# Graph attention over 25,000 edges: node pairs placed in the edge pipeline's first slots, small tables loaded in parts, and the segment sum in two passes

## What is computed

```
q = (x @ Wq + bq); k = (x @ Wk + bk); v = (x @ Wv + bv)        # 8 heads of 32
e = edge_attr @ We
kj = k[src] + e
alpha = einsum('ehc,ehc->eh', q[dst], kj) / sqrt(32)
ea = exp(alpha - segment_max(alpha, dst)[dst])
alpha = ea / (segment_sum(ea, dst)[dst] + 1e-16)
out = segment_sum((v[src] + e) * alpha[:, :, None], dst) + (x @ Ws + bs)
result = layernorm(x + out)
```

## Time and profile before

| | |
|---|---|
| median of 3 runs | 1380.74 us |
| the profiled execution | 1379.87 us, of which the span from first to last instruction is 1377.7 us |
| mean granted TensorE clock | 0.978 |
| busy: PE / PEld | 1297.1 us (94%) / 1157.9 us (84%) |
| busy: DVE / POOL / ACT | 974.1 us (71%) / 807.3 us (59%) / 729.4 us (53%) |
| node part, PE | until about 381 us |
| edge part, PE | 392.9 to about 1338 us |

### The profile page before, as it was taken

One profiled execution on the slowest core, in us unless ns is written; L12 is line 12 of the kernel. 1 busy time (PEld: TensorE's weight loads), 2 busy tenths in 40 slices (PEclk: granted clock), 3 DMA queues, 4 the chain that ended last, 5 costly groups with the idle time before them and its releaser, 6 DMA issues.

```text
span 1377.7 us, 26634 instructions
## 1 busy us (share of the span) xinstructions
PE 1297.1 (94%) x8027; PEld 1157.9 (84%) x8027; DVE 974.1 (71%) x2950; ACT 729.4 (53%) x1972; POOL 807.3 (59%) x749
## 2 busy tenths in 40 slices
PE   5689999999969999999999999999999999999973
PEld 4568888888859999899999999999999999999962
DVE  4497777777747777777777777767777777777763
ACT  2345555555535555555655555555555555555540
POOL 1123222222275677677777777777777777777542
PEclk9799999999989999999999999999999999999995
DMA  6769888888763344444444444444445444444310
GB/s 160 215 213 325 307 304 305 305 304 305 289 201 108 95 105 111 101 115 110 115 117 116 118 114 120 121 118 119 119 119 126 116 121 127 113 124 121 92 53 25
DMA packets 97231, 216.69 MB, mean 157 GB/s; under 512 B 31469, under 2 KB 35201, under 8 KB 97056
## 3 DMA queue, kind: packets, MB, share of 16 engines
q1 hardware_dynamic: 68672, 145.63, 33.1%
q0 software_dynamic: 28416, 69.35, 19.8%
HBM read 145.17 MB, written 77.90 MB: 162 GB/s over the span
## 4 chain that ended last, share of the span: by engine, by line
PE 91%; DVE 4%; DMA 3%; issue 1%; ACT 0%; POOL 0%; SPq 0%; POOLq 0%; DVEq 0%; ACTq 0%
PE bank L953 50%; PE bank L933 22%; PE bank L945 7%; PE bank L965 6%; PE bank L978 2%; PE bank L962 2%; DMA xT<-xt_dram 2%; DVE y L667 1%; PE bank L1022 1%; DVE y L681 1%; PE bank L990 1%; DVE at L653 1%; DMA rows_in<-xrows_dram,slot 1%; DMA bias<-bs_dram 1%; PE bank L984 0%
## 5 line engine op out<-in xcount | busy, mean ns | idle before, releaser
L403 POOL DMA_INDIRECT rows_in<-xrows_dram,slot x392 | 413.7, 1055 | 119.9 <-issue 94.6
L933 PE MATMUL bank<-w_y,xT 128*128 128x256 f32 x1568 | 345.9, 384 | 35.2 <-DMA xT<-xt_dram 15.9
L933 PEld LDWEIGHTS bank<-w_y,xT 128*128 128x128 f32 x1568 | 301.0, 193 | 79.7 <-DMA xT<-xt_dram 19.2
L953 PE MATMUL bank<-w_kv,sd 128*128 128x512 f32 x1176 | 341.2, 426 | 0.0
L419 POOL DMA_INDIRECT out_dram<-area,where x196 | 237.8, 1213 | 69.7 <-issue 44.4
L396 POOL TENSOR_TENSOR rstd<-var,half 128x4 f32<-128x4 f32 x98 | 99.0, 1010 | 283.4 <-DVE var L675 283.4
L953 PEld LDWEIGHTS bank<-w_kv,sd 128*128 128x128 f32 x1176 | 222.2, 190 | 45.1
L481 ACT ACTIVATE square<-y 128x256 f32<-128x256 f32 x392 | 159.7, 408 | 182.0 <-DVE var L675 79.1
L667 DVE TENSOR_TENSOR y<-bank,bias 128x512 f32<-128x512 f32 x196 | 135.2, 690 | 103.3 <-PE bank L933 98.8
L506 ACT COPY kv<-bank 128x512 f32<-128x512 f32 x196 | 115.1, 587 | 158.0 <-PE bank L953 156.2
L953 PE MATMUL bank<-w_q,sd 128*128 128x264 f32 x1176 | 191.3, 298 | 0.0
(11 more groups left out here) (117 smaller groups left out, 1528.3 us busy)
## 6 DMA issues: line engine op xcount, KB each, us to landing
xT<-xt_dram SPq DMA_DIRECT2D x98, 512.0 KB, 3.7
out_dram<-y SPq DMA_DIRECT2D x98, 512.0 KB, 3.4
eT<-et_dram SPq DMA_DIRECT2D x98, 256.0 KB, 2.9
dst_all<-dst_row_dram SPq DMA_DIRECT2D x49, 256.0 KB
rows_in<-xrows_dram,slot POOLq DMA_INDIRECT x392
bounds<-total SPq DMA_DIRECT2D x196, 0.1 KB
bounds<-peak SPq DMA_DIRECT2D x196, 0.1 KB
out_dram<-area,where POOLq DMA_INDIRECT x196, 2.4
```

The lines of the kernel that those rows point to most:

```text
L403: nc.gpsimd.indirect_dma_start(out=rows_in[:, t % RIN, i, :], out_offset=None, in_=xrows, in_offset=bass.IndirectOffsetOnAxis(ap=slot[:, t ...
L933: ins = nc.tensor.matmul(node_bank(u, b)[:, i * D:(i + 1) * D], xT[:, u % RX, c, 2 * b + i, :], w_y[:, c, :], start=(c == 0), stop=(c == K ...
L953: ins = nc.tensor.matmul(to, rows[a][:, c * P:(c + 1) * P], weights[b][:, c, :], start=(first and n == 0), stop=(last and n == len(terms) ...
```

## The change

**Node pairs in the edge slots.** The loop over 98 units becomes a loop over pairs. The first 16 pairs (`FRONT`), eight units, run ahead of the edge part. The other 180, with the steps that follow them, are handed out four to a slot (`PER_SLOT`) from slot -2 on, so that the last stands in slot 44. On PE they stand between `turn`, `aggregate`, the key/value product and the query product, which are now separate functions. In the front the pairs use four banks, afterwards two.

**The preparation.** `extras` starts at pair 8 with two items per pair and ends with pair 15; only the first of the seven flag steps is among them, the other six go to every other pair from 16 on. `load_rest` is issued in six parts, after pairs 1, 3, 5, 7, 9 and 11; three of the four bias broadcasts that stood at the start are now among them. `at` is bf16, and several small tables share memory with `area`. The stores are issued one unit later and `y` has five buffers.

**Scatters.** Since they may not start before the last node store, they begin in slot 47 and come at four in three slots until, in slot 145, they have caught up with tile `s - 14`; then it is one a slot. `zout` has 36 buffers, with 12 semaphores, and GpSimd waits for the scatter 12 tiles earlier before each.

**Segment sum.** `mv` is split like the other operands: ACT copies it rounded to fp32r (`high_mv`), DVE subtracts that and rounds the rest (`low_mv`), and PE multiplies `same`, now fp32r, with both parts: two fp32r matmuls in place of one full fp32 matmul.

```diff
@@ -32,18 +32,23 @@
 TINY = 1e-16
 SCALE = float(C) ** -0.5
-RX, RY = 3, 6
+RX, RY = 3, 5
 RIN = 6
 RQ, RK = 2, 2
 RD = 10
 RSAME = 10
 RV = 8
 RMV = 3
-RZ = 4
+RZ = 36
 LAG = 8
 FLAG_STEPS = 7
-assert EDGE_GROUPS % FLAG_STEPS == 0 and ENTRIES % EB == 0 and EW <= P
+FRONT = 16
+PER_SLOT = 4
+SIGNALS = 12
+SCATTER_FROM = 47
+LATE = 11
+assert RZ % SIGNALS == 0 and EDGE_GROUPS % FLAG_STEPS == 0 and ENTRIES % EB == 0 and EW <= P
...
-        node_units = range(NODE_GROUPS + 2)
         edge_slots = range(-2, TILES + LAG + 9)
+        PAIR_STEPS = 2 * NODE_GROUPS + 6
...
+        def pair_at(s, place):
+            p = FRONT + (s + 2) * PER_SLOT + place
+            return p if s >= -2 and p < PAIR_STEPS else None
+        def scattered_by(s):
+            return max(0, min(s - LAG - 5, (s - SCATTER_FROM + 1) * 4 // 3, TILES))
...
+        def extra(p):
+            if p >= FRONT:
+                n = 1 + (p - FRONT) // 2
+                return [("flags", n)] if p % 2 == 0 and n < FLAG_STEPS else []
+            k = (p - EXTRAS_FROM) * 2
+            return extras[k:k + 2] if k >= 0 else []
...
-            for i, b in enumerate((bk, bv, bq, bs)):
-                sp.dma_start(bias[:, i * D:(i + 1) * D], b.partition_broadcast(P)).then_inc(loaded_y, 16)
+            sp.dma_start(bias_s[:], bs.partition_broadcast(P)).then_inc(loaded_y, 16)
...
+            def load_rest(n):
+                if n == 0:
+                    load_weights(0, wk)
+                    load_weights(1, wv)
+                if n == 1:
+                    load_weights(2, wq)
+                    load_weights(3, we)
+                if n == 2:
+                    for i, b in enumerate((bk, bv, bq)):
+                        sp.dma_start(bias_kvq[:, i * D:(i + 1) * D], b.partition_broadcast(P)).then_inc(loaded_w, 16)
+                if n == 3:
+                    sp.dma_start(col_i, cols).then_inc(loaded_i, 16)
+                    for i in range(2):
+                        sp.dma_start(end_i[:, i, :], edge_ends[i].partition_broadcast(P)).then_inc(loaded_i, 16)
+                    sp.dma_start(slot[:].rearrange("p g j i -> p g (j i)"),
+                                 slots.rearrange("g p j i -> p g (j i)")).then_inc(loaded_i, 16)
+                if n == 4:
+                    for j in range(EG):
+                        sp.dma_start(target[j * H:(j + 1) * H].rearrange("h g e -> h (g e)"),
+                                     flag_rows[j].partition_broadcast(H)).then_inc(loaded_f, 16)
+                if n == 5:
+                    sp.dma_start(ent_i[:], entry_cols).then_inc(loaded_f, 16)
+                    sp.dma_start(erow_i[:], entry_row.partition_broadcast(P)).then_inc(loaded_f, 16)
...
-                if u == 1:
-                    load_rest()
-                if u >= 2:
-                    sp.wait_ge(node_rows, u - 1)
-                    sp.dma_start(out_groups[u - 2], y[:, (u - 2) % RY]).then_inc(stored[(u - 2) % RY], 16)
+                if u < 6:
+                    load_rest(u)
+                if u >= 3:
+                    sp.wait_ge(node_rows, u - 2)
+                    sp.dma_start(out_groups[u - 3], y[:, (u - 3) % RY]).then_inc(stored[(u - 3) % RY], 16)
...
-                scatter(s - LAG - 6)
-            for u in node_units:
-                node_unit(u)
+                for t in range(scattered_by(s - 1), scattered_by(s)):
+                    scatter(t)
+                for k in range(3):
+                    p = pair_at(s, k)
+                    if p is not None:
+                        node_pair(p)
...
+            def high_mv(t):
+                if not is_tile(t):
+                    return
+                act.wait_ge(mv_ready, t + 1)
+                over(act, z_mm, t - 1)
+                nc.scalar.copy(mv_part[0][:, t % 2, :], mv[:, t % RMV, :]).then_inc(mv_high, 1)
...
-                over(act, scattered[t % RZ], t // RZ * 16)
+                if t >= RZ:
+                    act.wait_ge(scattered[t % SIGNALS], ((t - RZ) // SIGNALS + 1) * 16)
...
+            def low_mv(t):
+                if is_tile(t):
+                    dve.wait_ge(mv_high, t + 1)
+                    over(dve, z_mm, t - 1)
+                    nc.vector.tensor_tensor(mv_part[1][:, t % 2, :], mv[:, t % RMV, :],
+                                            mv_part[0][:, t % 2, :].bitcast(F32), ALU.subtract).then_inc(mv_low, 1)
...
+                over(pe, biased, p - 3 if p < FRONT else p - 1)
...
-                nc.tensor.matmul(z_b[:, 0:D], same[:, t % RSAME, :], mv[:, t % RMV, :], start=False,
+                pe.wait_ge(mv_low, t + 1)
+                nc.tensor.matmul(z_b[:, 0:D], same[:, t % RSAME, :], mv_part[0][:, t % 2, :], start=False, stop=False)
+                nc.tensor.matmul(z_b[:, 0:D], same[:, t % RSAME, :], mv_part[1][:, t % 2, :], start=False,
                                  stop=True).then_inc(z_mm, 1)
...
+                def pair(place):
+                    if pair_at(s, place) is not None:
+                        node_pair(pair_at(s, place))
                 turn(s + 1)
+                pair(0)
                 aggregate(s - LAG)
-                project(s)
+                pair(1)
+                project_kv(s)
+                pair(2)
+                project_q(s)
                 for work, first in ((turn_alpha, 4), (turn_weights, 6)):
                     g = group_at(s, first)
                     if g is not None:
                         work(g)
-            for u in node_units:
-                node_unit(u)
-            pe.wait_ge(biased, NODE_GROUPS * 2)
+                pair(3)
...
```

More of the change, by code:

```diff
@@ L854, in edge_slot @@
                 low(s + 1)
+                if pair_at(s, 0) is not None:
+                    node_pair(pair_at(s, 0))
+                low_mv(s - 7)
                 compare(s)
```

216 lines of the change are left out of this document (119 added, 97 removed).

## The result

The changed kernel takes 1358.89 us (median of 4 runs, 1350.78 to 1362.23), beside 1380.84 us for the kernel before in the same session (4 runs, 1380.36 to 1382.05). The ratio is 0.9828, interval [0.9801, 0.9855]: 1.7% faster, where 0.9% was forecast. The ratios given with an interval leave out executions more than 1.5% above the fastest of their kernel and are not quotients of the medians (here that would be 0.984). The medians lie 22.0 us apart. The profiled execution is the quickest of the four, 1350.78 us with a span of 1348.9, so its gain on the kernel before, 28.8 us of span, is 7 us more than that of the medians.

What follows compares the result with a forecast made beforehand. PE, busy 1297.1 of 1377.7 us, bounds the kernel, with GpSimd 96% full in the edge part. 1377.7 - 38 - 33 - 3 + 2 + 60 = 1365.7 us of span, forecast 1368 us, 0.9% faster; range 1332 to 1391.

Steps and rivals of the forecast that it cites:

- The segment sum: Edge slots on PE: two fp32r matmuls save 0.195 us a slot, 38 us less; ACT and DVE work costed at nothing.
- The start: Start of the kernel: with one bias broadcast DVE can start near 5 us; 4.5 us less, bounds 0 and 7.
- The tables: Front: PE's stop on `xT` shrinks to some 8 us, `prepared` near 49 us; 33 us less by the first turn.
- DVE waits for the table in pair 12: Front: DVE waits there for the table of slots, the last preparation item for loads near 44, so `prepared` near 49 us.
- The change of part and the ramp: Node-to-edge change and first slots: pairs cover the first gather; 1.49 us for `sd` and the like lie beside pairs, 3 us less.
- The slots with pairs: Slots -2 to 44: PE stays the bound at 11.4 us a slot; 2 us more for waits with two banks.
- Rival 4: Slots with pairs lose half a microsecond each as PE waits for `biased`: 21 us more, 1389 us; chance 0.06.
- The scatters: From slot 47: crowded scatters make GpSimd the bound, 20.7 us a group against PE's 18.28; 60 us more.
- The rate of 0.6 us per us of work with two SBUF operands: GpSimd's issues: worst stretching by such DVE work; bounded `low_mv`'s effect at 1.0 us a group, 0.4 taken.
- The second: Rival: only the new subtraction is harmless to GpSimd, gathers 1.06 us as before; 14 us less, 1354 us; chance 0.2.
- The first rival: GpSimd is not the bound, 17.9 us a group under PE's 18.28; the 60 us fall away, 1308 us; chance 0.13.
- The fifth: Rival: the front gains nothing, table stops PE as before, `prepared` at 57; 8 us more, 1376 us; no chance given.

Runs made afterwards that it cites:

- experiment 2: Changed kernel with the old segment sum, one full fp32 matmul on unrounded mv, no high_mv or low_mv: 1376.09 us, ratio 0.9958; in an earlier session 1541.69 us, ratio 0.9933.
- experiment 3: Kernel before with only the two-pass segment sum, node pairs still ahead, one scatter a slot: 1358.74 us, ratio 0.9833; in an earlier session 1584.22 us, ratio 1.024.
- experiment 4: Changed kernel with the slot table in runs of 1568 bytes per partition in place of 49 short ones: 1554.72 us, ratio 1.004.
- experiment 5: Changed kernel with long slot-table runs and flag rows, entry tables, flag steps behind the first 12 pairs: 1354.05 us, ratio 0.9788; in an earlier session 1586.55 us, 1.0048.

## Why the prediction came out as it did

The range held the time and the sign was right. But 1368 against 1359 hides two large errors of opposite sign, and that they nearly cancelled was luck. In the profiled execution the first turn was forecast for 58 us and came at 69.3; PE was at turn 47 at 584.1 us, where the steps give about 563; and from turn 47 to turn 195 it took 701.0 us, where they give 738 (706.9 before, less 29 for the sum, plus 60). 21 us late and 37 us early make the 16 us between the forecast span, 1365.7, and 1348.9.

- **The segment sum, 38 us less.** The size per slot was right where PE is the bound (0.194 against 0.195, experiment 2). As a gain of the kernel it was 22.8 us alone: at 4.58 us a slot PE's share of busy time falls to 98.7%, and 0.07 us of each slot is lost (experiment 3). I costed it against a PE without any wait, and ACT's and DVE's part at nothing.
- **The start, 4.5 us less.** Right: PE's first matmul came at 8.71 us, 4.2 us earlier.
- **The tables, in the 33 us of the front.** The loss by the first turn, at which 20 pairs were done as forecast, fell from 56.4 to 69.3 - 34.3 = 35.0 us: 21.4 us of the 33. The step that failed is "DVE waits for the table in pair 12". It waits for the store of a unit, 10.7 us in two waits, where the kernel before had none. `prepared` came at 60.6 us, 11.6 later than forecast and outside my bounds of 36 and 57. The table was also not "as long as before": it held SP's queue for 4.80 us, not 13.58. The diff has two changes that explain the wait, the store issued a unit later and five `y` buffers for six: a store is now issued two units ahead of the pair that needs its buffer, four before, and two units are 6.9 us of PE's work against the 15.55 us that the store took. I had not followed the ring of `y`. No run gave the sixth buffer or the earlier store back, so this part is argued; experiment 4 shows that the table is not it, and experiment 5 that the wait returns later when the tables are moved.
- **The change of part and the ramp, 3 us less.** The gap is gone, but PE's turns 0 to 3 took 33.6 us. Before they took 10.8, and 12 pairs add 20.6: 2 us more, not 3 less. PE stood for 3.6 us behind GpSimd's ten gathers in a row and ran at a lower granted clock (0.91 from 60 to 100 us). I had not counted what the first gathers keep GpSimd from.
- **The slots with pairs, 2 us more.** Right: 11.482 us against 11.43, and no idle PE in 460 us. Rival 4 falls.
- **The scatters, 60 us more.** The mechanism is the one forecast: GpSimd without a wait for `vare`, DVE waiting for the power in `offsets`, PE behind it through `low`. Its size was 23 us by the same count (701.0 against 678.0), and 10 of these stand in the kernel with the two-pass sum alone as well (688.1, experiment 3), so the crowded scatters cost 13. Three terms were off. The scatter was priced at 1.227 us and took 1.080, 0.8 us a group; the subtraction was to add 0.4 us and added nothing (experiment 3); the power with the idle time ahead takes 1.08 us, not 1.2. With the changed kernel's own rows, 8 x 1.363 + 5.33 x 1.385 + 1.08 = 19.4 us is the group of the power's rows, 19.36. The error behind the first two: "The mean is the right one, because the stretching goes with what DVE does". In a kernel in lockstep that mean samples one phase. The median, 1.02 us, stands in the rows of all these kernels, and the earlier trace rows had it. It would not have been right either: by medians a group comes to 8 x 1.278 + 5.33 x 1.322 + 1.2 = 18.5 us, by means, without the subtraction, to the 20.3 that I had, and 19.36 was measured between them. The rate of 0.6 us per us of work with two SBUF operands had the same fault, since the long issues go with one of the three instructions, the scan (experiment 3).
- **The rivals.** The second, 1354 us, is the nearest, and its sign, gathers at 1.06 us as before, came (1.072). The rule of the Trainium skill ("SBUF — State Buffer", section "Who interferes with whom"), that `tensor_tensor` with two SBUF inputs contends only with GpSimd's reads and not with the writing of descriptors, agrees here for the subtraction: issues beside all of one take 1.07 us, and the group's issues in sum were no longer for 196 of them. The 1.81 us scatters don't speak against it as I had thought, since what goes with them is a scan, not a `tensor_tensor`; but issues beside all of the product in `messages`, which is one with both inputs in SBUF, take 1.21 us (31 of them, with the two-pass sum), so the rule isn't settled. The first rival, 1308, had GpSimd free; it is full from slot 48 to 145. The fifth, with `prepared` at 57 us, is the way the front went, and somewhat further.

The whole change and the two-pass sum alone take the same time by their medians. The node pairs in the slots bring PE to turn 47 15.5 us sooner than the two-pass sum alone does (584.1 against 599.6 in the profiled executions), and the scatters, crowded at 5.3 to a group, take 13.0 of these back by turn 145 (98 x (4.784 - 4.651)). This doesn't close the account. The profile of the changed kernel is its quickest execution and ends 7.8 us sooner than that of the two-pass sum, 5.2 of them behind turn 145, while the medians are equal. In which stretch the typical execution loses these 8 us no profile shows.

## What to carry to other kernels

Work that is moved to fill an engine's gaps takes the place of other work on the queues that shared the time: price what is now crowded, here the scatters on GpSimd, by the median of its rows and by their mean, and take both as bounds, since the mean of a kernel in lockstep repeats one coincidence and the median leaves all of them out. When a load is moved to free a queue, follow every ring of buffers whose transfers share the DMA engines, stores too; here a reordering only moved the wait. And time each part of a change alone before believing in their sum.

## What was not expected of the hardware

In two sessions the edge slots without pairs took 5.6 to 6.5 us in place of 4.8, with the same instructions. From 700 to 1000 us of one profile PE, DVE and ACT stood together ten times, for 2 to 5 us; ACT's waits there are for the sum of PE (L591), with no releaser that the profile can name ("remote"). The granted clock was lower too. From the run once more of the changed kernel, the waits from 560 to 1280 us and the stretch from 700 to 1000:

```profile
POOL rstd L455 <- DVE vare L897: 147.7, 27, 9.1
ACT area L591 <- remote: 75.3, 24, 5.8
```

```profile
700.00:1000.00 300.00, 243.55 (x1531) 214.48 (x1529) 181.09 (x557) 141.66 (x327) 181.36 (x172) 0.89 0.34 90
```

Slots with pairs were not touched, and the kernel without scatters little (4.90 us a slot, with 19 such waits of up to 3.1 us from 560 to 1280). The three sessions of the experiments ran on three different chips, so whether it is the session or the chip is open too. What holds PE in these stops, and why mostly where scatters are issued, the profile does not tell; it stays open. The two kernels with a two-pass sum and the one with a full sum also stood in another order there (1.0048, 1.024 and 0.9933) than in the undisturbed session (0.9828, 0.9833 and 0.9958), so a ranking made in such a session does not carry over.
